# Broadcast parameters from single elements through TensorE, quantization through byte tiles, and ring slots released by ScalarE

## The reference, cut to what matters

```python
def fake_quant(x, scale, zp):
    q = clip(round(x / scale + zp), 0, 255)
    return (q - zp) * scale

q1 = fake_quant(layernorm(x), x1_scale, x1_zp)        # per row of x
q2 = fake_quant(ctx, x2_scale, x2_zp)
x  = x + tanh(g_xattn) * (q1 @ q2)
y  = layernorm(x)
base = y @ W_base.T + b_base
gate = softmax(y @ W_gate.T); thr = sigmoid(y @ W_thr + b_thr) * 0.125
w    = max(gate - thr, 0);    w = w / (sum(w) or 1)    # 8 experts
moe  = (A_w-products of y, weighted by w) @ B_w * 2
x  = x + tanh(g_ffn) * (base + moe)
```

## Time and profile before

| what | value |
|---|---|
| time, median of 3 | 203.62 us (203.19 to 203.75) |
| profiled execution | 204.13 us, span 202.3 us from first to last instruction |
| PE busy | 176.5 us (87%) |
| DVE busy | 126.6 us (63%) |
| POOL busy | 89.6 us (44%) |
| ACT busy | 85.5 us (42%) |
| HBM read, written | 18.39 MB, 4.19 MB |

### The profile page before, as it was taken

How to read it: one execution, slowest core, us unless ns; L and a number is a source line. 1 busy time by engine, 2 the same in 40 slices (tenths; PEclk the granted TensorE clock), 3 DMA queues, 4 the chain that set the end, 5 groups by cost and what they waited for, 6 DMA issues and landing times.

```text
span 202.3 us, 3050 instructions
## 1 busy us (share of the span) xinstructions
PE 176.5 (87%) x1131; PEld 153.6 (76%) x1131; DVE 126.6 (63%) x268; ACT 85.5 (42%) x126; POOL 89.6 (44%) x127
## 2 busy tenths in 40 slices
PE   0072897989999899999997699999999999999992
PEld 0071752456889899999964247999999999999992
DVE  0594989998967977797999725562713503503303
ACT  2049992448495758487563011602420420400300
POOL 2185375477200568583776978528320310310310
PEclk9999699999999999999999999999999999999999
DMA  4759492999879000057002000000202002002002
GB/s 130 281 214 392 132 298 76 296 402 410 277 255 268 11 0 0 0 112 280 28 0 107 0 0 3 0 0 0 104 3 104 0 0 107 0 0 105 3 0 104
DMA packets 10464, 22.78 MB, mean 113 GB/s; under 512 B 1737, under 2 KB 3145, under 8 KB 10450
## 3 DMA queue, kind: packets, MB, share of 16 engines
q1 hardware_dynamic: 10162, 22.59, 32.2%
q10 hardware_dynamic: 288, 0.00, 0.1%
HBM read 18.39 MB, written 4.19 MB: 112 GB/s over the span
## 4 chain that ended last, share of the span: by engine, by line
PE 59%; DVE 20%; issue 6%; POOL 5%; ACT 4%; DMA 3%; SPq 1%; DVEq 0%; POOLq 0%
PE bank L914 15%; PE bank L915 15%; PE bank L916 15%; DVE q L602 6%; PE bank L807 3%; DMA prm<-in_L_xattn_x_scale_dram 3%; PE bank L902 3%; POOL colacc L356 3%; DVE WTl L631 2%; DVE q L604 2%; DVE st L575 2%; PE bank L935 2%; DVE xs L667 2%; PE bank L937 1%; DVE xs L617 1%
## 5 line engine op out<-in xcount | busy, mean ns | idle before, releaser
L914 PE MATMUL bank<-WTh,lnTh 128*128 128x388 f32 (+1 forms) x192 | 67.4, 351 | 0.0
L915 PE MATMUL bank<-WTl,lnTh 128*128 128x388 f32 (+1 forms) x192 | 65.2, 339 | 0.0
L916 PE MATMUL bank<-WTh,lnTl 128*128 128x388 f32 (+1 forms) x192 | 65.1, 339 | 0.0
L373 POOL TENSOR_TENSOR xs<-xs,tb 128x1024 f32<-128x1024 f32 x8 | 19.2, 2406 | 44.6 <-ACT xs L438 44.6
L914 PEld LDWEIGHTS bank<-WTh,lnTh 128*128 128x128 f32 x192 | 36.1, 188 | 0.7 <-DVE lnTl L631 0.2
L915 PEld LDWEIGHTS bank<-WTl,lnTh 128*128 128x128 f32 x192 | 36.2, 188 | 0.0
L916 PEld LDWEIGHTS bank<-WTh,lnTl 128*128 128x128 f32 x192 | 36.1, 188 | 0.0
L807 PE MATMUL bank<-q,q1T 128*128 128x512 bf16 x128 | 30.0, 382 | 2.2 <-DVE q L604 1.2
L356 POOL TENSOR_TENSOR colacc<-colacc,q 128x512 f16<-128x512 f16 x18 | 22.9, 1272 | 8.6 <-DVE q L604 7.8
L667 DVE SCALAR_TENSOR_TENSOR xs<-bank,con,xs 128x250 f32<-128x250 f32 (+2 forms) x24 | 12.6, 568 | 21.9 <-PE bank L937 16.3
L807 PEld LDWEIGHTS bank<-q,q1T 128*128 128x128 bf16 x128 | 12.0, 99 | 17.4 <-DVE q L604 3.1
(11 more groups left out here) (87 smaller groups left out, 244.7 us busy)
## 6 DMA issues: line engine op xcount, KB each, us to landing
ring<-in_ctx_dram SPq DMA_DIRECT2D x16, 512.0 KB, 5.8
xs<-in_x_dram SPq DMA_DIRECT2D x8, 512.0 KB, 7.8
ring<-in_L_ffn_W_base_dram SPq DMA_DIRECT2D x8, 512.0 KB, 6.3
out_dram<-xs SPq DMA_DIRECT2D x7, 512.0 KB, 2.7
tb<-in_L_ffn_b_base_dram SPq DMA_DIRECT2D x1, 512.0 KB, 5.6
ring<-in_L_ffn_A_w_dram SPq DMA_DIRECT2D x1, 512.0 KB, 4.8
ring<-in_L_ffn_B_w_dram SPq DMA_DIRECT2D x1, 512.0 KB, 6.3
out_dram<-xs SPq DMA_DIRECT2D x1, 194.0 KB, 2.2
```

The lines of the kernel that those rows point to most:

```text
L373: nc.gpsimd.tensor_tensor(xs[:, t, :], xs[:, t, :], tb[:, :], ALU.add).then_inc(xb_ready, 1)
L914: mm(o, hi, WTh[:, k, a:b], start=(k == 0), stop=False, skip_group_check=True)
L915: mm(o, hi, WTl[:, k, a:b], start=False, stop=False, skip_group_check=True)
L916: ins = mm(o, lo, WTh[:, k, a:b], start=False, stop=(k == KT - 1), skip_group_check=True)
```

## The change

1. The seven parameters are loaded as single elements into one partition (`prow`, in the memory of `rt`), all on ACT's queue. A row of ones (in the memory of `gt`) times this row, a product with K = 1 on PE, spreads them over 128 partitions in PSUM; DVE copies them to `prm`. SP's queue holds only the four x tiles ahead of the ring.
2. ACT writes the scaled values as bytes (`q1u`, two buffers; `q2u`, three), so that the conversion rounds and clips. One DVE operation (minus 128, byte to bfloat16) replaces the two roundings.
3. A ctx slot of the ring is given back when ACT has read it (`ctx_affine`) instead of when DVE has rounded it.
4. `work` has two buffers, for `normalise` alone. `affine_q1(t)` from t = 2 waits for `round_q1(t - 2)`; `affine_ctx(c)` from c = 3 waits for `round_ctx(c - 3)`. The statistics buffer `st` is used for both layer norms.

```diff
-    NW = 3
+    NW = 2
+    NU = 3
...
+        q1u = sb("q1u", [P, 2, D], U8)
+        q2u = sb("q2u", [P, NU, 2 * H], U8)
...
-        st = sb("st", [P, 2, T, 2, 6])
+        st = sb("st", [P, T, 2, 6])
...
+        prow = rt[0:1, :]
+        ones_row = gt[0:1, :, :].rearrange("p a b -> p (a b)")
...
                     if old[0] == "ctx":
-                        sp.wait_ge(q2_ready, old[1] + 1)
+                        sp.wait_ge(ctx_affine, old[1] + 1)
...
-            load_x(0)
-            load_x(1)
-            for i, p in enumerate((x1_scale, x2_scale)):
-                sp.dma_start(prm[:, 2 * i:2 * i + 1], p.rearrange("(a d) -> a d", a=1).to_broadcast([P, 1])
-                             ).then_inc(s_scales, 16)
-            for t in range(2, MT):
+            for t in range(MT):
                 load_x(t)
-            for i, p in enumerate((g_x, g_f, b_thr)):
-                sp.dma_start(prm[:, 4 + i:5 + i], p.rearrange("(a d) -> a d", a=1).to_broadcast([P, 1])
-                             ).then_inc(s_param, 16)
...
+            nc.gpsimd.memset(ones_row[:, :], 1.0).then_inc(ones_ready, 1)
...
-            pool.wait_ge(s_scales, 4 * 16)
             pool.wait_ge(s_recip, 1)
...
-            for i, p in enumerate((x1_zp, x2_zp)):
-                act.dma_start(prm[:, 2 * i + 1:2 * i + 2], p.rearrange("(a d) -> a d", a=1).to_broadcast([P, 1])
-                              ).then_inc(s_scales, 16)
...
+            for i, p in enumerate((x1_scale, x1_zp, x2_scale, x2_zp)):
+                act.dma_start(prow[:, i:i + 1], p.rearrange("(a d) -> a d", a=1)).then_inc(s_scales, 16)
+            for i, p in enumerate((g_x, g_f, b_thr)):
+                act.dma_start(prow[:, 4 + i:5 + i], p.rearrange("(a d) -> a d", a=1)).then_inc(s_param, 16)
 
             def affine_q1(t):
-                w = work_free(("q", t))
+                if t >= 2:
+                    act.wait_ge(q1_ready, t - 1)
                 act.wait_ge(coefs[0], t + 1)
-                nc.scalar.activation(w, xs[:, t, :], ACT.Identity, bias=cf[:, 0, t, 4:5],
+                nc.scalar.activation(q1u[:, t % 2, :], xs[:, t, :], ACT.Identity, bias=cf[:, 0, t, 4:5],
                                      scale=cf[:, 0, t, 3:4]).then_inc(q1_affine, 1)
 
             def affine_ctx(c):
                 arrived(act, ("ctx", c))
                 s = ring[:, slot_of["ctx", c], :]
-                nc.scalar.activation(s, s, ACT.Identity, bias=Z2, scale=R2).then_inc(ctx_affine, 1)
+                if c >= NU:
+                    act.wait_ge(q2_ready, c - NU + 1)
+                nc.scalar.activation(q2u[:, c % NU, :], s, ACT.Identity, bias=Z2, scale=R2).then_inc(ctx_affine, 1)
...
-            act.wait_ge(s_param, 3 * 16)
+            act.wait_ge(s_prm, 2)
...
             def round_q1(t):
                 dve.wait_ge(q1_affine, t + 1)
-                w = work[:, work_no["q", t] % NW, :]
-                q = q1[:, t % 2, :]
-
                 if t >= 2:
                     dve.wait_ge(flipped, flip_no["q1", t - 2] + 1)
-                link(nc.vector.tensor_scalar(q, w, ROUND, ROUND + CENTRE, ALU.add, ALU.subtract))
-                nc.vector.tensor_scalar(q, q, QMAX - CENTRE, -CENTRE, ALU.min, ALU.max).then_inc(q1_ready, 1)
+                nc.vector.tensor_scalar(q1[:, t % 2, :], q1u[:, t % 2, :], -CENTRE, None, ALU.add).then_inc(q1_ready, 1)
...
-                link(nc.vector.tensor_scalar(q, s.rearrange("p (k n) -> p k n", k=2),
-                                             ROUND, ROUND + CENTRE, ALU.add, ALU.subtract))
-                nc.vector.tensor_scalar(q, q, QMAX - CENTRE, -CENTRE, ALU.min, ALU.max).then_inc(q2_ready, 1)
+                nc.vector.tensor_scalar(q, q2u[:, c % NU, :].rearrange("p (k n) -> p k n", k=2),
+                                        -CENTRE, None, ALU.add).then_inc(q2_ready, 1)
...
             ln_moments(0, 0)
-            dve.wait_ge(s_scales, 4 * 16)
+            dve.wait_ge(scales_spread, 1)
+            link(nc.vector.tensor_copy(prm[:, 0:4], bank[1][:, 256:260]))
             nc.vector.reciprocal(R1, S1).then_inc(s_recip, 1)
             nc.vector.reciprocal(R2, S2).then_inc(s_recip, 1)
+            dve.wait_ge(params_spread, 1)
+            nc.vector.tensor_copy(prm[:, 4:7], bank[2][:, 0:3]).then_inc(s_prm, 2)
             for t in range(1, MT):
                 ln_moments(0, t)
...
+            pe.wait_ge(ones_ready, 1)
+            pe.wait_ge(s_scales, 4 * 16)
+            mm(bank[1][:, 256:260], ones_row[:, :], prow[:, 0:4], start=True, stop=True).then_inc(scales_spread, 1)
+            pe.wait_ge(s_param, 3 * 16)
+            mm(bank[2][:, 0:3], ones_row[:, :], prow[:, 4:7], start=True, stop=True).then_inc(params_spread, 1)
             pe.wait_ge(s_ident, 3 + 2 * (GP > G))
             pe.wait_ge(coefs[0], 1)
             keep_busy(32)
```

More of the change, by code:

```diff
@@ L21 @@
 FP16 = mybir.dt.float16
+U8 = mybir.dt.uint8
 ALU = mybir.AluOpType
@@ L26 @@
 P = 128
-ROUND = 12582912.0
-QMAX = 255.0
 CENTRE = 128.0
@@ L116, in gated_block @@
     own_col_adds = [(0, 0, 0), (0, 1, 0)]
-    works = [("q", t) for t in range(MT)] + [("n", 0), ("n", 1), ("n", 2), ("q", MT), ("q", MT + 1), ("n", 3)]
-    works += [("q", MT + 2), ("q", MT + 3)] + [("n", t) for t in range(MT, T)]
-    work_no = {key: n for n, key in enumerate(works)}
     es = ExitStack()
@@ L170, in gated_block @@
         s_bias = sem("s_bias")
+        ones_ready = sem("ones_ready")
+        scales_spread = sem("scales_spread")
+        params_spread = sem("params_spread")
+        s_prm = sem("s_prm")
         x_loaded = [sem(f"x_loaded{t}") for t in range(T)]
@@ L467, in normalise @@
             def normalise(t):
-                w = work_free(("n", t))
+                if t >= NW:
+                    act.wait_ge(flipped, flip_no["ln", t - NW, 1] + 1)
+                w = work[:, t % NW, :]
                 act.wait_ge(coefs[1], t + 1)
@@ L574, in half_stats @@
                         dve.wait_ge(cols_added, col_adds.index((b, h, m)) + 1)
-                nc.vector.bn_stats(st[:, i, t, h, :], xs[:, t, h * H:(h + 1) * H]).then_inc(dve_step, 1)
+                nc.vector.bn_stats(st[:, t, h, :], xs[:, t, h * H:(h + 1) * H]).then_inc(dve_step, 1)
                 n_step[0] += 1
@@ L581, in ln_moments @@
                 dve.wait_ge(dve_step, n_step[0])
-                nc.vector.bn_aggr(mv[:, i, t, :], st[:, i, t, :, :].rearrange("p a b -> p (a b)")).then_inc(moments[i], 1)
+                nc.vector.bn_aggr(mv[:, i, t, :], st[:, t, :, :].rearrange("p a b -> p (a b)")).then_inc(moments[i], 1)
             def round_q1(t):
                 dve.wait_ge(q1_affine, t + 1)
-                w = work[:, work_no["q", t] % NW, :]
-                q = q1[:, t % 2, :]
                 if t >= 2:
                     dve.wait_ge(flipped, flip_no["q1", t - 2] + 1)
-                link(nc.vector.tensor_scalar(q, w, ROUND, ROUND + CENTRE, ALU.add, ALU.subtract))
-                nc.vector.tensor_scalar(q, q, QMAX - CENTRE, -CENTRE, ALU.min, ALU.max).then_inc(q1_ready, 1)
+                nc.vector.tensor_scalar(q1[:, t % 2, :], q1u[:, t % 2, :], -CENTRE, None, ALU.add).then_inc(q1_ready, 1)
             def round_ctx(c):
@@ L596, in round_ctx @@
                 dve.wait_ge(ctx_affine, c + 1)
-                s = ring[:, slot_of["ctx", c], :]
                 q = q2[:, 2 * k2:2 * k2 + 2, h * H:(h + 1) * H]
@@ L685, in _ @@
             round_ctx(1)
-            dve.wait_ge(s_param, 3 * 16)
             dve.wait_ge(s_tanh, 2)
@@ L897, in flip_ln @@
                 pe.wait_ge(ln_ready, t + 1)
-                s = work[:, work_no["n", t] % NW, :]
+                s = work[:, t % NW, :]
                 for i in range(NH):
```

## The result

The changed kernel takes 196.58 us (196.47 to 196.93, four runs) beside 203.67 us of the kernel before (203.19 to 203.75): a ratio of 0.966, 95% interval 0.9640 to 0.9679, or 7.1 us. The forecast was 195.4 us in a range of 193.4 to 199.0, a gain of 8.2 us. The profiled span went from 202.3 to 194.4 us.

What follows compares the result with a forecast made beforehand. PE is nearly always busy, so gains come only from the start up to the weight transposes (5.2 us) and the second product's stalls (3.0 of 3.4 us): 203.62 - 8.2 = 195.4 us, range 193.4 to 199.0.

Steps and rivals of the forecast that it cites:

- The last parameter at 7.3 us: Start: last single-element load lands at 7.3 us, between bounds 5.6 and 9.1, so statistics of tile 1 start at 7.9.
- late parameters: Rival, start: last parameter lands at 9.1 us, moving DVE's statistics and ACT's third tile by 1.8; 197.2 us, chance 0.15.
- POOL's coefficients of tile 2 at 12.65: Start, POOL: coefficients of tile 2 ready by 12.65 us, as DVE's roundings no longer fall on them.
- ACT's list, 8.6 us to the last copy: Front, ACT: from third q1 tile at 12.9 us to last q1 copy at 21.5, 8.6 us where 9.07 before.
- The product behind it, 11.4 us from the row sums to the transposes: Front, first product: PE is the bound for 11.4 us from 22.8, so weight transposes start at 34.2.
- POOL ends 0.6 us before PE asks: Second product: POOL's adds end at 112.3, PE asks at about 112.9, so the third stall (1.93 us) goes.
- column sums still late: Rival, second product: POOL's adds stay last to arrive, gain there only 1.5 us; 196.9 us, chance 0.08.
- Byte roundings at 0.69 us, byte tiles on ACT at 1.23: Quantization: one DVE rounding from bytes takes 0.69 us, ACT's byte output 1.23 us; DVE loses about 10 us of work.
- The low clock: Rival, first product: PE runs 3.4 us at half clock inside it, losing 1.7 us; 197.1 us, chance 0.08.
- Slow reads: Rival, DVE: byte reads at one element a cycle, each rounding 1.23 us; 196.0 us, chance 0.06.
- slow bytes: Rival, front: ACT's byte tiles cost more; at twice 1.23 us the front loses 12 us, 208 us; chance 0.04.
- Slots and earlier loads counted at nothing: Ring: slots given back by ACT bring loads some microseconds earlier, but no engine waits for them; counted as nothing.

Runs made afterwards that it cites:

- params_only: Kernel before with only the change's single-element parameter loads, two spreading products and copies; 202.75 us, ratio 0.9964.
- slow_free: Changed kernel with the ctx rounding in a form that also sums over the row, plus a wait for the previous rounding; 195.91 us, ratio 0.9610.
- double_loads: Changed kernel with each of the seven single-element parameter loads made twice and PE waiting for all; 199.66 us, ratio 0.9784.
- params_later: Changed kernel with DVE's wait for the last three parameters, and their copy, moved behind the statistics of tiles 1 to 3; 195.38 us, ratio 0.9598.
- hold_rounding: Changed kernel with a third q1 buffer and the first rounding held back until POOL's coefficients of tile 2 are there; 195.80 us, ratio 0.9615.
- three_buffers: Changed kernel with a third buffer for q1 (tile 2 uses one of ctx's), no rounding held back; 196.23 us, ratio 0.9646.
- sums_behind_chunk: Changed kernel with the last column sum moved behind the first chunk of the second half of batch 1's product; 195.93 us, ratio 0.9628.
- slots_dve: Changed kernel with ring slots given back after DVE's rounding, as before the change; 196.34 us, ratio 0.9645.

## Why the prediction was right, and where its steps were not

The time lay in the range and the mechanism of the sum held in outline: 5.2 us in the front (4.95 measured up to the weight transposes), 3.0 in the second product (2.80), nothing between (0.25, as the first float32 product of tile 0 moved from 50.53 to 45.33) and nothing behind (0.1 lost). That the front came out so close is partly luck: one step in it was 0.9 us too good, and others were too bad. The steps one by one:

- *The last parameter at 7.3 us.* Measured 7.14 in this execution, 7.8 in `params_only` and 7.6 in `slow_free`: right, though by two errors that cancel. The seventh load was issued at 2.72, not 3.39, and took 4.42 us to land, not 3.9. Statistics of tile 1 at 7.9: measured 7.96. x tile 0 came earlier (3.95), not at the 5.6 assumed, and POOL began at 6.85 instead of 7.7; neither helped, since the wait behind it absorbed both. The rule of the Trainium skill on single-element loads ("DMA: Bandwidth & Descriptors", section "Why a DMA increments its semaphore by 16 and not by 1"), by which all seven share one engine, fits the 0.5 us that each load adds, without being the only reading of it; its feared effect on x, that tiles wait for that engine, the runs do not show. The rival "late parameters" did not happen, but what it rests on holds: `double_loads` delayed the last parameter by 3.6 us and the third tile by as much. The prediction had the new wait in its 7.9 and did not ask what it costs: with the wait out of DVE's way, in `params_later`, 1.2 us more come out.
- *POOL's coefficients of tile 2 at 12.65, "since DVE's roundings no longer fall on them".* This step failed. DVE's first rounding started at 12.18, on the last two thirds of the chain, and stretched it to 13.73. It was the largest error of the front, 0.9 us, and `hold_rounding` shows it. (POOL began 0.85 us sooner than assumed but then stood 1.03 us for DVE's statistics of tile 1, so the start of the chain does not explain the error.) The new buffer wait, to which the prediction gave this place, ended before and cost nothing (`three_buffers`).
- *ACT's list, 8.6 us to the last copy.* Measured 8.44.
- *The product behind it, 11.4 us from the row sums to the transposes.* Measured 10.9, from 23.58 to 34.49: 0.5 us better, which paid half of the error above and was not foreseen. The kernel before lost more in that stretch than the one stall of 1.17 us that the prediction had counted: the 12 products behind it took 3.16 us, 0.26 each, where 32 of them now take 7.07, 0.22 each.
- *Which part brings it.* The prediction's order of steps, third tile 2.7 sooner and then 2.5 us on the way to the transposes, made the parameters the larger half of the front. Measured alone the parameters bring 1.0 and the bytes 3.8. The rounding pass was worth more in the front, because its removal also takes away the 0.5 us idle on ACT, lets PE's chunks follow the copies and shortens POOL's stretched coefficients: with the old parameters the third tile still moved from 15.59 to 14.94.
- *Second product: POOL ends 0.6 us before PE asks.* This step failed too: PE stands 0.93 us for it. POOL's start was 0.5 us later than assumed (92.53 is 97.73 on the old axis, 5.20 later; 97.2 was assumed), and the adds took 15.5 us instead of the 15.05 that the old ones were busy, as many were still held up by a rounding beside them (1.50 us instead of 1.16). The rival "column sums still late" described what happened to this stall, at half its price. That 2.80 of the forecast 3.0 came all the same is luck again: the prediction took the three stalls, 3.4 us, for all there was, but `sums_behind_chunk` is 3.67 and `slow_free` 3.90 us below the kernel before in this stretch.
- *Byte roundings at 0.69 us, byte tiles on ACT at 1.23.* Alone 0.68 and 1.24; DVE lost 13.7 us of work in all, not about 10. The table of the Trainium skill that gives a scalar operation four elements a cycle on bfloat16 in SBUF and two on float32 ("VectorE: DVE Perf Modes", section "The perf-mode tier table (the rule you actually need)") has no row for bytes; the prediction's reading of it agrees with the 0.68 us for 1024 bytes, the float32 value and not the 0.43 of the two-byte pass.
- *The other rivals.* The low clock did not fall inside the product: the granted clock was 0.50 from 18 to 20 us, 0.84 from 20 to 22 and 1.00 behind that, and most of the product stands there. Slow reads and slow bytes are excluded by the 0.68 and 1.24 us.
- *Slots and earlier loads counted at nothing.* `slots_dve`: right.
- *From profile to median.* The profiled executions give 7.7 us (204.13 to 196.47), the medians 7.1. The prediction carried the 0.5 us by which the old profiled execution stood above its median over to the new kernel, whose profiled execution stood 0.1 below. The three kernels with two roundings all stood 0.45 to 0.6 above, the others between 0.4 below and 0.25 above. Why is open.

Of the 1.2 us between forecast and result, then, 0.6 is this last term. The span shrank by 7.9 us instead of 8.2, which is 0.3 more, and the remaining 0.2 lies between span and time of the profiled execution (1.8 us before, 2.1 after).

The mutual stretch of DVE and POOL has a rule in the Trainium skill ("SBUF — State Buffer", section "SBUF: two separate sides"): the two share a pair of ports that one instruction of either holds until its end; an instruction of DVE takes it only in a two-port mode or with two inputs in SBUF. `slow_free` agrees: the form at 1.21 us keeps its time whatever POOL does, and POOL's adds run at 1.16.

## What to carry to other kernels

Price a DVE pass by what waits behind it and by whom it holds up, not by its own 0.43 us. Where DVE and POOL hand the same data on and hold each other up, a removed pass gives time on both, here 6 us for 24 passes. When a load is moved or split, look at the wait that comes with it and at what is queued behind that wait; here a wait for three values that nobody needed for 11 us (ACT's tanh at 19.04) cost 1.2 us, more than the whole part brought, and moving it behind work that was ready was free. After a producer gets faster, expect the next engine in the chain to become the last to arrive. Add up its busy time with nothing between, at the durations it has beside the other engines, and compare that with the moment when its result is wanted. And when a wait is moved away, look for the next consumer of the same engine: here 0.3 of 0.87 us came back one tile later.

## What the hardware showed that was not expected

- Single-element loads from one queue, beside a bulk load, land about 0.5 us apart although they are issued 0.3 us apart: PE could use the fourth at 5.8 us, the seventh landed at 7.14, the fourteenth of fourteen at 10.7. (From the fourth to the seventh it is 0.3 to 0.7 us for each in the other executions.)
- POOL's operations on one element per partition, 0.19 us alone, take 0.52 and 0.71 us when a DVE rounding of 1024 elements runs beside them, and 0.19 again when it is held back.
- A DVE form nearly twice as slow alone (1.21 beside 0.68 us) left the kernel no slower, as it neither waited for POOL nor held it up.
- ACT writes bytes, which here take the place of rounding and clipping on DVE, at the price of float32 (1.24 us beside 1.23 for 1024 elements in each partition).
